# Combine gathers five batches ahead, the last fold loads issued before the last stores, tables and keys held for the first combine

## The reference

```python
x = x + _L0_xattn_ref(_layernorm(x), ctx_512, ...)       # 16 heads, causal
x = x + _L0_ffn_ref(_layernorm(x), Wg, W1, W2, W3)       # 8 experts, top 2
x = x + _L1_xattn_ref(_layernorm(x), ctx_512, ...)       # rotated keys, 16 heads
x = x + _L1_ffn_ref(_layernorm(x), ...)                  # weights and rows rounded to 8 bits

# _L0_ffn_ref: two experts for each token, weighted by a softmax of their scores
for e in range(E):
    h = silu(x @ W1[e].T) * (x @ W2[e].T)
    y = y + w[..., e:e + 1] * (h @ W3[e].T)
# _L1_xattn_ref, the part that is folded
q_hk  = (hidden_q @ Wq.T).reshape(b, s, H, K)
q_big = einsum('bshk,hkq->bshq', q_hk, w_kc_q)
q_r   = einsum('bshq,hqr->bhsr', q_big, W_qr)
```

## Time and profile before

| | us |
|---|---|
| median of three runs | 973.84 |
| lowest and highest run | 968.15, 975.36 |
| the profiled execution | 971.65 |
| its span, first to last instruction | 970.0 |
| TensorE busy | 801.4 |
| VectorE busy | 466.9 |
| ScalarE busy | 370.3 |
| GpSimd busy | 232.2 |
| TensorE's share of the chain that ended last | 53% |

### The profile page before, as it was taken

One profiled execution on the slowest core, in us unless ns is written; L12 is line 12 of the kernel. 1 busy time (PEld: TensorE's weight loads), 2 busy tenths in 40 slices (PEclk: granted clock), 3 DMA queues, 4 the chain that ended last, 5 costly groups with the idle time before them and its releaser, 6 DMA issues.

```text
span 970.0 us, 14470 instructions
## 1 busy us (share of the span) xinstructions
PE 801.4 (83%) x4668; PEld 608.2 (63%) x4668; DVE 466.9 (48%) x1083; ACT 370.3 (38%) x773; POOL 232.2 (24%) x300
## 2 busy tenths in 40 slices
PE   0789888784999999986989989899877999867774
PEld 0677776582555555585978778787744777645552
DVE  4544335442101111146564663745645666678872
ACT  2432223210212111122474663755743444454441
POOL 1400000002101110053082460732612122223432
PEclk9887888855999999985899999999999999978987
DMA  8300000282465664373000010010046343200000
GB/s 265 154 1 2 0 0 1 77 349 97 140 208 192 192 201 152 109 217 105 1 23 32 32 41 22 31 41 23 35 164 240 109 131 108 73 1 17 17 18 17
DMA packets 28620, 88.24 MB, mean 91 GB/s; under 512 B 6004, under 2 KB 9276, under 8 KB 26272
## 3 DMA queue, kind: packets, MB, share of 16 engines
q1 hardware_dynamic: 23104, 70.49, 21.2%
q0 software_dynamic: 5472, 17.18, 5.9%
HBM read 72.57 MB, written 15.07 MB: 90 GB/s over the span
## 4 chain that ended last, share of the span: by engine, by line
PE 53%; issue 18%; DVE 14%; POOL 6%; DMA 5%; ACT 3%; SPq 0%; POOLq 0%; DVEq 0%; ACTq 0%
PE PS L1028 10%; PE PS L146 8%; PE PS L148 7%; PE PS L147 7%; PE PS L1044 6%; POOL wraw L648 4%; PE PS L1414 2%; PE PS L1110 2%; PE PS L1397 2%; DMA raw<-wkv_in 1%; DMA fq_raw<-foldq_in 1%; DVE ht L1449 1%; PE PS L1095 1%; DVE xn L126 1%; DVE mx L1538 1%
## 5 line engine op out<-in xcount | busy, mean ns | idle before, releaser
L648 POOL TENSOR_TENSOR wraw<-wraw,rinv 128x361 f32<-128x361 f32 (+1 forms) x104 | 80.7, 787 | 140.2 <-DVE rinv L1595 140.1
L1028 PE MATMUL PS<-w,xt 128*128 x320 | 100.7, 468 | 1.5 <-ACT xt L734 1.5
L1028 PEld LDWEIGHTS PS<-w,xt 128*128 128x128 f32 x320 | 61.9, 194 | 41.7 <-issue 12.8
L1449 DVE COPY ht<-PS 128x384 f32<-128x384 f32 x20 | 11.2, 558 | 145.1 <-PE PS L1036 145.1
L825 ACT ACTIVATE wraw<-PS,nmx 128x361 f32<-128x361 f32 (+1 forms) x104 | 58.6, 564 | 37.8 <-DVE nmx L1602 29.8
L1602 DVE TENSOR_REDUCE nmx<-PS 128x1 f32<-128x361 f32 (+1 forms) x104 | 55.0, 530 | 34.0 <-PE PS L148 33.4
L1044 PE MATMUL PS<-w,ht 128*128 128x512 f32 (+1 forms) x120 | 56.9, 610 | 5.1 <-DVE ht L1449 5.1
L1605 DVE TENSOR_TENSOR pt_lo<-PS,pt_hi 128x384 fp32r<-128x384 f32 x96 | 52.3, 546 | 11.6 <-ACT pt_hi L831 10.8
L1209 PE MATMUL PS<-ident,wraw 128*128 128x128 f32 x312 | 52.0, 276 | 6.1 <-POOL wraw L648 3.4
L146 PE MATMUL PS<-pf_hi,cx_hi 128*100 128x512 f32 x128 | 51.7, 404 | 4.1 <-DVE pf_lo L1732 4.1
L600 POOL DMA_INDIRECT xb<-xn_scratch,rows x20 | 19.1, 953 | 137.2 <-PE PS L1019 134.1
(11 more groups left out here) (255 smaller groups left out, 2018.7 us busy)
## 6 DMA issues: line engine op xcount, KB each, us to landing
w<-w_in SPq DMA_DIRECT2D x20, 768.0 KB, 4.8
w<-w_in SPq DMA_DIRECT2D x8, 1408.0 KB, 10.6
fq_raw<-foldq_in SPq DMA_DIRECT2D x6, 1088.0 KB, 7.3
cx_raw<-ctx_scratch SPq DMA_DIRECT2D x8, 800.0 KB, 5.6
ctx_scratch<-ctxo SPq DMA_DIRECT2D x24, 256.0 KB, 2.0
wraw<-wup_in POOLq DMA_DIRECT2D x22, 256.0 KB
ys_scratch<-yb SPq DMA_DIRECT2D x20, 256.0 KB, 4.9
wraw<-wdown_in POOLq DMA_DIRECT2D x4, 704.0 KB
```

Of the source, the lines that this page charges most:

```text
L648: pool.tensor_tensor(P1[slot][0:rows, 0:NK], P1[slot][0:rows, 0:NK], rinv[0:rows, jj, t:t + 1].broadcast_to((rows, NK)), ALU.mult).then_in ...
L1028: last = pe.matmul(PS[:, which, 0:FH], XT[i % 2][:, k * 128:(k + 1) * 128], w12_of(e, which, k), start=(k == 0), stop=(k == KC - 1))
```

## The change

Four edits. The ring of gather buffers goes from three batches to five (ten buffers; the last two lie at another place), and the semaphores of the gathers of ring places 3 and 4 are those that the expert blocks' own gathers had used (their count starts at 160, YBASE). GpSimd's wait and VectorE's wait follow the new ring. The loads of fold weights 6 and 7 are issued behind the store of block 17 and in front of the stores of blocks 18 and 19, with a wait for E["ups"] at 20 in place of that for the first gathers. The tables and keys get a wait for E["x"] at 2, the combine of batch 0.

```diff
+YRING = 5
@@
-        YG = [at(f"yg{i}", [T, D], YG_AT + 4 * D * i) for i in range(6)]
+        YG = [at(f"yg{i}", [T, D], YG_AT + 4 * D * i if i < 8 else 2 * FQB + 4 * D * (i - 8)) for i in range(TOPK * YRING)]
@@
-                      "w12 xs0 xs1 w30 w31 xtp xt gps ups silu h htp ht yps yb ys0 ys1 x")
+                      "w12 xs0_yg3 xs1_yg4 w30 w31 xtp xt gps ups silu h htp ht yps yb ys0 ys1 x")
         YGS = [W[f"yg{i}_ld{i}"] for i in range(3)]
-        LD0 = [16 * TOPK * len(range(i, B, 3)) for i in range(3)]
-        XS, W3S = [E["xs0"], E["xs1"]], [E["w30"], E["w31"]]
+        LD0 = [16 * TOPK * len(range(i, B, YRING)) for i in range(3)]
+        XS, W3S = [E["xs0_yg3"], E["xs1_yg4"]], [E["w30"], E["w31"]]
+        YSEM, YBASE = YGS + XS, [0] * 3 + [16 * NBLK // 2] * 2
@@
                 load_block(i)
                 store_block(i - 2)
+            sp.wait_ge(C["fq1"], 32)
+            sp.wait_ge(E["ups"], NBLK)
+            for k in range(6, NP1):
+                sp.dma_start(FQR[k][:, :, :], foldq_d[k]).then_inc(C["fq1"], 16)
             store_block(NBLK - 2)
             store_block(NBLK - 1)
-            sp.wait_ge(C["fq1"], 32)
-            sp.wait_ge(YGS[0], 16 * TOPK)
-            for k in range(6, NP1):
-                sp.dma_start(FQR[k][:, :, :], foldq_d[k]).then_inc(C["fq1"], 16)
+            sp.wait_ge(E["x"], 2)
             sp.dma_start(cosr[:, :, :], cos_d).then_inc(C["cs"], 16)
             sp.dma_start(sinr[:, :, :], sin_d).then_inc(C["cs"], 16)
@@
             for b in range(B):
-                wait(pool, E["x"], TOPK * (b - 2))
+                wait(pool, E["x"], TOPK * (b - YRING + 1))
                 for k in range(TOPK):
-                    pool.indirect_dma_start(YG[TOPK * (b % 3) + k][:, :], None, ys_scratch,
-                                            bass.IndirectOffsetOnAxis(ap=slots[:, k, b:b + 1], axis=0)).then_inc(YGS[b % 3], 16)
+                    pool.indirect_dma_start(YG[TOPK * (b % YRING) + k][:, :], None, ys_scratch,
+                                            bass.IndirectOffsetOnAxis(ap=slots[:, k, b:b + 1], axis=0)).then_inc(YSEM[b % YRING], 16)
@@
             for b in range(B):
-                dve.wait_ge(YGS[b % 3], 16 * TOPK * (b // 3 + 1))
+                dve.wait_ge(YSEM[b % YRING], YBASE[b % YRING] + 16 * TOPK * (b // YRING + 1))
                 for k in range(TOPK):
-                    g = TOPK * (b % 3) + k
+                    g = TOPK * (b % YRING) + k
```

## The result

| | before | after |
|---|---|---|
| median of 14 runs, us | 974.5 | 977.5 |
| the profiled execution, us | 971.65 | 977.35 |
| its span, us | 970.0 | 975.5 |
| start of the first gather, us | 413.38 | 412.24 |
| TensorE's M6, us | 431.19 | 433.74 |

The ratio of the times is 1.0036, with a 95% interval of 1.002 to 1.0053: the changed kernel is a third of a percent slower, where 962 us was forecast. One of the 14 runs of the kernel before took 1934.94 us, and the ratio leaves it out.

A forecast was written before the change was run, and what follows sets the result against it. TensorE's DMA wait for fold weights 6 and 7 (M6 late by 4.57 us), then half clock, was taken as the bound. Gain 10.8 us: 971.65 gives 960.9, the median 973.84 gives 963.0; forecast 962, range 956 to 970.5.

The forecast's parts named there:

- The loads: Fold loads 6 and 7 on SP's queue: issued at about 402.3 and 402.7, through at about 409.5, at worst 414.7.
- The stores behind them: Stores of blocks 18 and 19 on SP's queue: 0 to 1 us late, upper bound 4.5, hidden by 3.1 us of slack.
- The gathers: Sixteen on GpSimd, 1.31 us apart from 413.38: last starts at 433.0, last pair lands at 437.0, wanted at 440.1.
- TensorE then goes on without a gap: TensorE's folds after M6 at 426.6: M7 at 429.75, N6 at 431.1, N7 at 432.9, done at 434.85.
- no gain beyond the 11.1: The deeper gather ring adds nothing to the 11.1 us from the first aggregate coming at 442.3, not 453.47.
- ScalarE's 4.04 us: Unexplained "remote" idle time before ScalarE's copy of fold 2; if it stays, the gain is 10.3 us, not 11.1.
- The clock: TensorE's clock in the folds: stays at 1.00, as in the 17.50 us of the same matmuls before the stall.
- the clock falls in the folds though nothing stalls: Rival for TensorE's folds: from M6 on the 15.66 us stay, only 4.57 us of lateness go; 969 us, chance 0.06.
- Combines and the tail: VectorE behind the folds: 6.0 us from fold 7's low part to the first aggregate, 442.3; TensorE's restart at 444.6.
- The last pair: Last two gathers: land at 437.0, 3.1 us before VectorE wants them; without the deeper ring not that early.
- Tables and keys: Loads on SP's queue held for the first combine: 2 us later, landed by 436; cost nothing, cover 5 us.

## Why the prediction was wrong

- **The loads.** Through at about 409.5 was said, 409.0 measured. Right.
- **The stores behind them.** A delay of 0 to 1 us was said; GpSimd was idle for 10.66 us before the first gather against 10.65 in the earlier trace rows. None. The rule weighed there against the change (stores behind a big load in the ring wait for it) agrees with the store of block 18, issued at 405.53 behind the loads: it took 4.1 us to land, against 2.0 in the kernel before, and landed at 409.6, after them. It cost nothing, since the loads had landed before the last store was issued at 409.4, and that one took 2.0 us and set the start of the gathers.
- **The gathers, and with them "TensorE then goes on without a gap".** This step failed. The gathers were said to be 1.31 us apart with "no gain beyond the 11.1" and costed at nothing but their own arrival. They were mostly 1.29 to 1.51 us apart, but at that rate a run of more than four or five holds up ScalarE, and then TensorE: M6 at 433.74 and not at 425.5, 8.3 us late. From there the last five pieces of the folds took 15.6 us at half clock and not 8.2, another 7.3 us: the last fold was done at +37.1, where the prediction had +21.5. The prediction looked at what waits for a gather, and not at what a gather does to engines that don't wait for it.
- **The hint was in the rows.** ScalarE's 4.04 us were seen and priced with their own 0.8 us, on the guess that "the loads leave this stretch, so it may shrink". They came from the gathers, and the change makes just these runs longer: from 8 without a long pause to 14. A stall that nothing explains should have had its cause among the things that the change makes more of.
- **The clock.** "I take it that it does" stay, on condition of unbroken matmuls. With unbroken matmuls it does (1.00 to the last fold in the kernel with early loads alone). In the changed kernel TensorE was busy 1.85 of 3.20 us from 427.3 on and the clock was 0.50. The rival "the clock falls in the folds though nothing stalls" named the right clock for the wrong reason, since here TensorE stalled before the clock fell; its 969 us wasn't reached either.
- **Combines and the tail.** The sum for them was right where the gathers were out of the way: last fold at +21.47 said, +21.42 measured with one pair of gathers; restart at +31.2 said, +31.9 measured.
- **The last pair.** It was said to need the ring of five to be early enough. In the kernel with early loads and a ring of three the last gather is issued at 434.73, VectorE's folds being earlier too, and VectorE doesn't wait for it. The edit wasn't needed.
- **Tables and keys.** No cost was said. They don't cause the harm; whether their wait costs up to 1.5 us in the tail isn't settled.

The forecast of 10.8 us was for the early loads. Counted from the first gather, they brought the restart forward by 7.1 us alone (42.05 - 34.93), by 7.2 and 8.3 us with the gathers paced, and by 10.1 us with one pair only; the ratios of those that compute everything are 0.994, 0.987 and 0.990. So the gain of the load order was there, a few microseconds of it held back by the gathers that have to be made, and it was turned into a loss by the edit that was costed at nothing. The ring of five alone, without the early loads, gives that loss in full (1.003, restart at +45.7).

## What to carry to other kernels

Gathers issued by GpSimd aren't free for engines that never touch their data: at one per 1.31 us, a run of more than four or five slowed ScalarE and, when it went on, TensorE, until a microsecond after it ended, and one per 1.64 us did nothing. When a ring of buffers is made deeper, ask what the issuer will now do in one go, and leave the ring as it was or pace it by the consumer (one wait on a counter that runs anyway was enough here: 0.987 against 1.004). And idle time marked "issue" or "remote" that nothing explains belongs to something; find out to what before costing a change that does more of what lies beside it.

## What the runs showed of the hardware

- Fourteen indirect DMAs issued mostly 1.29 to 1.51 us apart by GpSimd cut TensorE down to three or four matmuls per 1.43 us and ScalarE to one instruction per 4.3 us. VectorE's instructions kept their pace where they had their operands: at 425.70, 426.31 and 426.91 us, the first of them 0.04 us behind ScalarE's copy.
- The harm goes by the number of gather instructions in time: half the rows in each, 1.22 to 1.24 us apart, gave more of it (last fold at +40.4), the same bytes by SP's plain DMAs none, and 28 memsets on GpSimd none.
- It begins anew in each run: on ScalarE at about the fifth gather (what was ready at 417.82 us, 5.6 us after the first, started at 420.72), on TensorE later (its first gap that no wait explains is the 0.71 us before 423.63, 11.4 us after the first), and it ended a microsecond after the run of 14. 1.36 us apart is harmful, 1.64 us isn't, and a mean of 1.55 us is nearly harmless.
- A busy DMA system isn't it: at a share of 1.06 TensorE was undisturbed, at 0.56 it was busy 1.21 us of three.
- What the engines are short of isn't shown. That it is the supply of instructions is read from idle time marked "issue" inside a group of matmuls without a wait; the queues marked "instruction" moved nothing unusual in that time, and through which path GpSimd's gathers do it is open.
